# Splitting the four index scatters of a token tile around the softmax product on GpSimd

## Chip, cores and metric

One core of one Trainium2 chip. The metric is the device time of one execution of the whole kernel in microseconds (us). Three timed runs of the kernel before gave 1762.08, 1763.48 and 1767.51 us; the median is 1763.48 us.

## The reference

Two residual blocks follow each other on 16 x 1024 tokens of width 512.

```python
x = x + attention(layernorm(x), ctx)   # 8 heads of 64, 64 context rows a batch, softmax over the rows
x = x + ffn(layernorm(x))              # 32 experts, top 4 by sigmoid score + bias, capacity 512 each,
                                       # weights normalised over the 4, plus a shared gated ffn
```

The part that matters here: every token is filed under its four experts in a table of slots (32 experts x 512 places), from which the expert stage later gathers its rows. The softmax of a tile needs, for each of 8 heads, the exponentials of 64 scores divided by their sum.

## The kernel before, in words

The 16,384 tokens are 128 tiles of 128. The kernel has a token stage, which is a software pipeline of steps n = 0 to 136, and an expert stage behind it. In a step every engine runs a fixed list of pieces, each for another tile: a piece with the lag L works on tile n - L. Each engine takes its list in order, and semaphores order the engines against each other. No planner is involved; the order within a step is the order in which the step function of each engine is written.

The pieces of one step that matter, by engine (the lags are the constants at lines 59 to 61):

- TensorE (PE): the scores of tile n-8 into S_ps (L485), the mix of tile n-10 into O_ps from the transposed probabilities pt_h and pt_l (L500), the router logits of tile n-14 (L517); twice in a group of four tiles the upper half of the shared ffn (L527) and twice its lower half (L537), and parts of the folded weights (L583, L599).
- ScalarE (ACT): the high part xt_h of the turned input of tile n-7 (L758), the rows x and x_h of tile n-13 (L846, L858), the first guess of an inverse root (L862), the high part p_h of the probabilities of tile n-9 (L788), the exponentials prob of tile n-8 (L799).
- VectorE (DVE): in even steps the first piece of a root iteration (L1033, a tensor_scalar on four elements a lane) at the head of the step; the low parts x_l of tile n-13 (L1221) and p_l of tile n-9 (L1227), the row maxima (L1280), the difference from them (L1286), the sums of the exponentials (L1298) and their reciprocals rsum of tile n-8 (L1314), then pieces of the shared ffn (L1084, L1089, L1116) and of the routing.
- SyncE (SP): the DMA queue. In a step it turns x_h and x_l (L397), then p_h and p_l (L404).
- GpSimd (POOL): first the low part xt_l of tile n-7 (L932); in two of four steps the low part ht_l of the shared ffn's hidden rows (L940), which the lower half of that ffn on PE and VectorE's next copy stand beside; then four indirect DMAs (L923), one for each of the four expert slots of each token of tile n-20; then the product prob = prob x rsum of tile n-8 (L947).

The function `file(t, first, end)` issues the indirect DMAs of the slots first to end-1 of tile t. The first DMA of a group of four tiles waits until the slots of the group are there (`slots_ready`). The product waits for `rsum_done`.

In the text below, steps are told apart by n mod 4. The group pieces fall as follows: ht_l on GpSimd in steps with n mod 4 of 2 and 3; the slot list of the next group (L1199, L1206, L1211, L1212) on VectorE in mod 3 (L1199 at its head); the residuals of the shared ffn (L1116) at the end of mod 3 and mod 0; the root's first piece L1033 at the head of mod 0 and mod 2. In some steps with mod 3 PE also projects keys and values for a later pair of batches (L566, function `kv`); between step 23 and step 131 there are 28 steps with mod 3, 12 with that job and 16 without it. Those 16, with the mod 0 step behind each, are called free pairs below.

Of the kernel before, what the change touches and what calls it, by code (L numbers as in the profile page):

```python
# [36 lines left out]
E, TOP, CAP, I = 32, 4, 512, 256  # L37
# [23 lines left out]
ROUTE, MEMBERS, SLOTS_AT, WEIGHTS, OUT, W_STORE, TABLE = 17, 18, 19, 20, 20, 21, 20  # L61
# [9 lines left out]
def at(n, lag):  # L71

    t = n - lag
    return t if 0 <= t < TILES else None


def group_at(n, lag):

    g = (n - lag) // 4
    return g if (n - lag) % 4 == 0 and 0 <= g < GROUPS else None  # L80
# [42 lines left out]
def after(eng, sem, count):  # L123

    if count > 0:
        eng.wait_ge(sem, count)
# [8 lines left out]
def tokens_and_experts(nc, x, xT, ctxT, wqT, wk, wv, wo, bo, gateT, bias, w1, w3, w2, sw1T, sw3T, sw2T, out, x2aug, table):  # L135
    stack = ExitStack()
    with stack:
# [201 lines left out]
        with nc.Block() as block:  # L339
# [571 lines left out]
            def _(pool):  # L911
                def file(t, first, end):
                    if t is None:
                        return
                    g, i = t // 4, t % 4
                    if i == 0 and first == 0:
                        if g == 0:
                            pool.wait_ge(fill_stored, (2 * PAD // P + 1) * 16)
                            pool.wait_ge(const_set, 11)
                        pool.wait_ge(slots_ready, 2 * g + 2)  # L920
                        pool.sem_inc(passed, 1)
                    for q in range(first, end):
                        pool.indirect_dma_start(  # L923
                            table, bass.IndirectOffsetOnAxis(ap=slot[:, g % 2, i, q:q + 1], axis=0),
                            tok_line[:, g % 2, i, :], None, bounds_check=SLOTS - 1, oob_is_err=False).then_inc(scattered[g % 2], 16)

                def step(n):
                    t = at(n, XT_SPLIT)
                    if t is not None:
                        pool.wait_ge(xt_hi, t + 1)  # L930
                        after(pool, scores_done, t - 1)
                        pool.tensor_tensor(xt_l[:, t % 2, :, :], xt[:, t % 2, :, :], xt_h[:, t % 2, :, :].bitcast(F32),  # L932
                                           ALU.subtract).then_inc(xt_lo, 1)
                    for c in range(2):
                        g = group_at(n, FFN_UP + c + 1)
                        if g is not None:
                            pool.wait_ge(ht_hi, g * 2 + c + 1)
                            after(pool, g_done, g * 4)
                            after(pool, u_done, g * 4)
                            pool.tensor_tensor(ht_l[:, c, :], hid[:, :], ht_h[:, c, :].bitcast(F32),  # L940
                                               ALU.subtract).then_inc(ht_lo, 1)
                    if n != FINAL + SCORES:
                        file(at(n, TABLE), 0, TOP)
                    t = at(n, SCORES)
                    if t is not None:
                        pool.wait_ge(rsum_done, t + 1)
                        pool.tensor_tensor(prob[:, t % 2, :, :], prob[:, t % 2, :, :],  # L947
                                           rsum[:, :].unsqueeze(2).to_broadcast([P, H, SKV]), ALU.mult).then_inc(prob_done, 1)
                    if n == FINAL + SCORES:
                        file(at(n, TABLE), 0, TOP)  # L950

                pool.memset(zrow, 0.0).then_inc(zero_set, 1)
                pool.memset(kbd[:, :, :, :], 0.0).then_inc(zero_set, 1)
# [24 lines left out]
                for n in range(TAIL):  # L978
                    step(n)
# [819 lines left out]
```

## Time and profile before

| | us |
|---|---|
| median of the three timed runs | 1763.48 |
| span of the profiled execution, first to last instruction | 1810.0 |
| token stage with filing, about | 130 to 1250 |
| last tiles, change of stage, about | 1250 to 1370 |
| expert stage, about | 1370 to 1810 |

The profiled execution is the only one whose instructions are seen. For it no time is shown apart from the span; the span is 46.5 us, 2.6%, above the median of the timed runs. Rows of instructions read: start, duration, engine, line, operation, out<-in; in brackets the idle time of the engine before it and who ended it.

### The profile page before, as it was taken

How to read it: one execution, taken by the hardware profiler on the slowest of the kernel's cores; microseconds unless marked ns; L12 is line 12 of the kernel's file. 1: busy time of each engine (PE TensorE's matmuls, PEld its weight loads, DVE VectorE, ACT ScalarE, POOL GpSimd, SP SyncE). 2: the span in 40 equal slices, each digit the busy share in tenths (PEclk: the TensorE clock that was granted, in tenths of full speed). 3: DMA queues.
4: the chain of work that ended last, by engine and by line, in shares of the span. 5: the costliest groups of instructions: out<-in, count | busy, mean ns of one | idle time of the engine just before them, and what ended most of it. 6: DMA issues, size and time to landing. Idle time of an engine off the chain costs nothing.

```text
span 1810.0 us, 31933 instructions
## 1 busy us (share of the span) xinstructions
PE 1641.8 (91%) x9056; PEld 1023.7 (57%) x9056; DVE 1378.9 (76%) x3486; ACT 1066.3 (59%) x2368; POOL 1252.4 (69%) x1104
## 2 busy tenths in 40 slices
PE   6999999999999999999999999999447999999991
PEld 4565656666566665656666565655224555555550
DVE  4678988987898897889779789898425777777771
ACT  4777766776776676777767767765213444444440
POOL 2337777777777777777767677777475787777874
PEclk8999999999999999999999999999678999999996
DMA  7557876667776666677666577777249889988665
GB/s 247 144 135 166 193 163 151 174 155 154 181 183 152 162 168 155 174 167 178 164 149 170 152 182 171 161 191 170 61 142 264 139 172 166 208 190 167 103 85 79
DMA packets 474532, 293.75 MB, mean 162 GB/s; under 512 B 342643, under 2 KB 385397, under 8 KB 474356
## 3 DMA queue, kind: packets, MB, share of 16 engines
q1 hardware_dynamic: 429300, 239.03, 51.9%
q0 software_dynamic: 45056, 52.67, 18.5%
q8 instruction: 74, 1.21, 0.3%
q14 instruction: 102, 0.84, 0.2%
HBM read 135.06 MB, written 110.17 MB: 135 GB/s over the span
## 4 chain that ended last, share of the span: by engine, by line
PE 45%; issue 17%; DVE 16%; ACT 9%; another core or an unknown queue 4%; DMA 3%; POOL 2%; SPq 2%; DVEq 0%; ACTq 0%; POOLq 0%
PE O_ps L500 9%; PE S_ps L485 8%; PE GE_ps L1580 5%; PE UE_ps L1580 4%; PE G_ps L527 4%; PE YE_ps L1620 4%; PE U_ps L527 3%; PE PREP_ps L583 2%; POOL out L1557 2%; PE PREP_ps L566 2%; DVE top_s L1280 2%; DVE x_l L1221 1%; DMA pt_l<-p_l 1%; PE TE_ps L1606 1%
## 5 line engine op out<-in xcount | busy, mean ns | idle before, releaser
L923 POOL DMA_INDIRECT slot_table<-tok_line,slot x480 | 507.7, 1058 | 132.0 <-issue 128.1
L932 POOL TENSOR_TENSOR xt_l<-xt,xt_h 128x512 fp32r<-128x512 f32 x128 | 164.6, 1286 | 179.5 <-ACT xt_h L758 179.5
L799 ACT ACTIVATE prob<-S_ps,rs 128x512 f32<-128x512 f32 x128 | 88.0, 688 | 257.3 <-DVE S_ps L1286 166.5
L485 PE MATMUL S_ps<-a_h,xt_h 128*128 128x512 f32 x512 | 213.3, 417 | 2.4 <-DVE m_l L1259 2.4
L500 PE MATMUL O_ps<-m_h,pt_h 128*128 128x512 f16 x512 | 195.9, 383 | 20.0 <-DMA pt_l<-p_l 18.9
L485 PE MATMUL S_ps<-a_h,xt_l 128*128 128x512 f32 x512 | 202.1, 395 | 0.0
L485 PE MATMUL S_ps<-a_l,xt_h 128*128 128x512 f32 x512 | 202.0, 395 | 0.0
L500 PE MATMUL O_ps<-m_h,pt_l 128*128 128x512 f16 x512 | 194.7, 380 | 0.0
L500 PE MATMUL O_ps<-m_l,pt_h 128*128 128x512 f16 x512 | 194.6, 380 | 0.0
L947 POOL TENSOR_TENSOR prob<-prob,rsum 128x512 f32<-128x512 f32 x128 | 135.4, 1058 | 83.0 <-DVE rsum L1314 62.3
L1557 POOL DMA_INDIRECT out<-ye,idx_far x80 | 126.3, 1579 | 52.2 <-issue 27.7
L485 PEld LDWEIGHTS S_ps<-a_h,xt_h 128*128 128x128 f32 x512 | 98.1, 192 | 37.4 <-issue 16.1
L1672 ACT ACTIVATE xe_h<-TE_ps 128x512 f16<-128x512 f32 x128 | 75.8, 593 | 67.7 <-PE TE_ps L1606 51.6
L1654 ACT ACTIVATE the<-GE_ps 128x512 f32<-128x512 f32 x64 | 38.2, 597 | 126.7 <-PE GE_ps L1580 90.5
L1221 DVE TENSOR_TENSOR x_l<-x,x_h 128x512 f16<-128x512 f32 x126 | 86.4, 685 | 33.4 <-ACT x_h L858 26.7
L1620 PE MATMUL YE_ps<-down_w,he_h 128*128 128x512 f32 x256 | 110.8, 433 | 0.6 <-DVE he_l L1712 0.6
L485 PEld LDWEIGHTS S_ps<-a_h,xt_l 128*128 128x128 f32 x512 | 97.5, 190 | 21.9
L500 PEld LDWEIGHTS O_ps<-m_h,pt_h 128*128 128x128 f16 x512 | 49.9, 97 | 102.9 <-issue 29.5
L485 PEld LDWEIGHTS S_ps<-a_l,xt_h 128*128 128x128 f32 x512 | 98.0, 191 | 17.3
L1606 PE MATMUL TE_ps<-ident_r,rows 128*128 128x128 f32 x512 | 67.2, 256 | 43.9 <-DVE xe_l L1718 34.1
L846 ACT ACTIVATE x<-xr,nb,rs 128x512 f32<-128x512 f32 x128 | 102.8, 803 | 1.0 <-DVE nb L1045 1.0
L1700 DVE SCALAR_TENSOR_TENSOR gte<-the,GE_ps 128x512 f32<-128x512 f32 x64 | 44.0, 688 | 77.5 <-ACT the L1654 49.8
(245 smaller groups left out, 4848.8 us busy)
## 6 DMA issues: line engine op xcount, KB each, us to landing
xt<-in_xT SPq DMA_DIRECT2D x128, 256.0 KB
xr<-in_x SPq DMA_DIRECT2D x64, 512.0 KB, 3.8
x2aug<-x SPq DMA_DIRECT2D x128, 256.0 KB
out<-xr SPq DMA_DIRECT2D x64, 512.0 KB, 3.2
up_more<-in_w SPq DMA_DIRECT2D x36, 256.0 KB
slot_table<-tok_line,slot POOLq DMA_INDIRECT x512
up_w<-in_w SPq DMA_DIRECT2D x28, 256.0 KB
down_more<-in_w SPq DMA_DIRECT2D x18, 256.0 KB
```

The costliest lines, as they stand in the source:

```text
L485: last = pe.matmul(S_ps[t % 2][:, :], left[:, kc, :], right[:, b % 2, kc, :], start=(m == 0), stop=(m == 3 * KD - 1))
L500: last = pe.matmul(O_ps[:, :], left[:, t % 2, p, :], right[:, b % 2, p, :], start=(m == 0), stop=(m == 3 * PAIRS - 1))
L527: last = pe.matmul(bank[:, :], up_sb[:, kc, w0 + c * P:w0 + (c + 1) * P], part[:, g % 2, kc, :], start=(m == 0), stop=(m == 2 * KD - 1))
L799: act.activation(prob[:, t % 2, :, :], S_ps[t % 2][:, :].rearrange("p (h j) -> p h j", h=H), ACT.Exp, scale=rs[:, q % 2, 0, t % 2:t % 2 + ...
L846: act.activation(x2[:, t % 2, :], x_tile(t), ACT.Identity, bias=nb2[:, q % 2, t % 2:t % 2 + 1], scale=rs[:, (q + LATER) % 2, 1, t % 2:t % ...
L923: pool.indirect_dma_start(table, bass.IndirectOffsetOnAxis(ap=slot[:, g % 2, i, q:q + 1], axis=0), tok_line[:, g % 2, i, :], None, bounds_ ...
L932: pool.tensor_tensor(xt_l[:, t % 2, :, :], xt[:, t % 2, :, :], xt_h[:, t % 2, :, :].bitcast(F32), ALU.subtract).then_inc(xt_lo, 1)
L947: pool.tensor_tensor(prob[:, t % 2, :, :], prob[:, t % 2, :, :], rsum[:, :].unsqueeze(2).to_broadcast([P, H, SKV]), ALU.mult).then_inc(pro ...
L1221: dve.tensor_tensor(split_rows(t)[1][:, :], x2[:, t % 2, :], split_rows(t)[0][:, :], ALU.subtract).then_inc(x2_lo, 1)
L1557: pool.indirect_dma_start(out, bass.IndirectOffsetOnAxis(ap=index(e, c), axis=0), ye[:, e % 4, c, :], None, bounds_check=TOKENS + PAD - 1, ...
L1580: last = pe.matmul(bank[:, :], up_set(e)[:, kc, w0 + c * P:w0 + (c + 1) * P], part[:, e % TURNED, kc, :], start=(n == 0), stop=(n == 2 * K ...
L1620: last = pe.matmul(YE_ps[i % 2][:, :], part[:, e % 2, c, i * P:(i + 1) * P], down_w[:, e % 2, c, :], start=(n == 0), stop=(n == 2 * KI - 1))
```

## The change

GpSimd's list in a step is cut differently. Two of the four indirect DMAs of tile n-20 stay ahead of the product of tile n-8, the other two are issued behind it, and so stand ahead of the next step's xt_l. The one step in which all four stood behind the product (n = FINAL + SCORES = 135) stays as it is. Nothing is removed or added: the same instructions with the same operands and the same semaphores.

```diff
@@ -940,7 +940,7 @@
                             pool.tensor_tensor(ht_l[:, c, :], hid[:, :], ht_h[:, c, :].bitcast(F32),
                                                ALU.subtract).then_inc(ht_lo, 1)
                     if n != FINAL + SCORES:
-                        file(at(n, TABLE), 0, TOP)
+                        file(at(n, TABLE), 0, 2)
                     t = at(n, SCORES)
                     if t is not None:
                         pool.wait_ge(rsum_done, t + 1)
@@ -948,6 +948,8 @@
                                            rsum[:, :].unsqueeze(2).to_broadcast([P, H, SKV]), ALU.mult).then_inc(prob_done, 1)
                     if n == FINAL + SCORES:
                         file(at(n, TABLE), 0, TOP)
+                    else:
+                        file(at(n, TABLE), 2, TOP)
```

## Rows read from the trace of the kernel before

**Rows 1.** Windows, us 130 to 1250: PE, PEld, DVE, ACT, POOL, clock, DMA.

```profile
130.00:1250.00 1120.00, 1096.15 (x6232) 686.83 (x6231) 960.89 (x2701) 786.35 (x1845) 827.27 (x748) 1.00 0.70 168
```

**Rows 2.** Waits of PE in that window: us in total, times, longest.

```profile
PE O_ps L500 <- DMA pt_l<-p_l: 12.0, 14, 1.6
```

**Rows 3.** Groups by line: busy us, mean ns, idle before, releaser.

```profile
L788 ACT ACTIVATE p_h<-prob 128x512 f16<-128x512 f32 x128 | 78.5, 613 | 0.0
```

**Rows 4.** Timeline of GpSimd, end of step 70 and step 71.

```profile
628.83 0.97 POOL L923 DMA_INDIRECT slot_table<-tok_line,slot  x1 [0.30 <-issue]
629.80 1.08 POOL L947 TENSOR_TENSOR prob<-prob,rsum 128x512 f32<-128x512 f32 x1
631.67 1.28 POOL L932 TENSOR_TENSOR xt_l<-xt,xt_h 128x512 fp32r<-128x512 f32 x1 [0.79 <-ACT xt_h L758]
632.90 1.28 POOL L940 TENSOR_TENSOR ht_l<-hid,ht_h 128x512 fp32r<-128x512 f32 x1
```

**Rows 5.** Timeline of VectorE in the same stretch.

```profile
628.67 0.19 DVE L1314 RECIPROCAL rsum<-sums 128x8 f32<-128x8 f32 x1
...
633.37 0.86 DVE L1211 COPY tok_line<-tok 128x64 int32<-128x64 int32 x1
...
634.22 0.68 DVE L1221 TENSOR_TENSOR x_l<-x,x_h 128x512 f16<-128x512 f32 x1
```

**Rows 6.** Timeline of GpSimd, step 39.

```profile
318.63 1.28 POOL L932 TENSOR_TENSOR xt_l<-xt,xt_h 128x512 fp32r<-128x512 f32 x1 [1.89 <-ACT xt_h L758]
```

**Rows 7.** Timeline of GpSimd, end of step 71 and step 72.

```profile
639.61 1.08 POOL L947 TENSOR_TENSOR prob<-prob,rsum 128x512 f32<-128x512 f32 x1
640.61 1.30 POOL L932 TENSOR_TENSOR xt_l<-xt,xt_h 128x512 fp32r<-128x512 f32 x1
642.07 1.01 POOL L923 DMA_INDIRECT slot_table<-tok_line,slot  x1 [0.17 <-issue]
```

**Rows 8.** Timeline of VectorE in the same stretch.

```profile
638.26 0.20 DVE L1314 RECIPROCAL rsum<-sums 128x8 f32<-128x8 f32 x1
...
639.62 2.33 DVE L1033 TENSOR_SCALAR nt<-mv 128x4 f32<-128x4 f32 x1
...
642.52 0.67 DVE L1221 TENSOR_TENSOR x_l<-x,x_h 128x512 f16<-128x512 f32 x1
643.12 0.15 DVE L1036 TENSOR_TENSOR nt<-rs 128x4 f32<-128x4 f32 x1
```

**Rows 9.** Timeline of ScalarE in the same stretch.

```profile
641.26 0.63 ACT L858 ACTIVATE x_h<-x 128x512 f16<-128x512 f32 x1
```

**Rows 10.** Line L1033: ns shortest/median/longest, first and last start.

```profile
L1033 DVE TENSOR_SCALAR nt<-mv x67: 159/915/2346, 25.4 to 1289.9; 128x4 f32<-128x4 f32 x67
```

**Rows 11.** Timeline of VectorE and GpSimd, end of step 72.

```profile
647.35 0.19 DVE L1314 RECIPROCAL rsum<-sums 128x8 f32<-128x8 f32 x1
...
647.63 1.04 POOL L947 TENSOR_TENSOR prob<-prob,rsum 128x512 f32<-128x512 f32 x1 [0.73 <-issue]
```

**Rows 12.** Timeline of GpSimd and VectorE, step 131.

```profile
1214.43 1.27 POOL L940 TENSOR_TENSOR ht_l<-hid,ht_h 128x512 fp32r<-128x512 f32 x1
...
1214.45 1.29 DVE L1212 TENSOR_SCALAR slot<-slot_f 128x16 int32<-128x16 f32 x1
```

**Rows 13.** Timeline of GpSimd and VectorE, step 133.

```profile
1230.05 1.31 POOL L932 TENSOR_TENSOR xt_l<-xt,xt_h 128x512 fp32r<-128x512 f32 x1
...
1230.93 0.98 DVE L1221 TENSOR_TENSOR x_l<-x,x_h 128x512 f16<-128x512 f32 x1 [1.40 <-ACT x_h L858]
```

**Rows 14.** Timeline of VectorE and GpSimd, step 83.

```profile
746.89 0.29 DVE L1199 TENSOR_TENSOR over<-taken,member 128x128 f32<-128x128 f32 x1
...
746.96 1.38 POOL L932 TENSOR_TENSOR xt_l<-xt,xt_h 128x512 fp32r<-128x512 f32 x1 [0.72 <-ACT xt_h L758]
```

**Rows 15.** Timeline of PE: first product of the mix, steps 41 and 72.

```profile
335.83 0.39 PE L500 MATMUL O_ps<-m_h,pt_h 128*128 128x512 f16 x1 [0.77 <-DMA pt_l<-p_l]
...
641.37 0.39 PE L500 MATMUL O_ps<-m_h,pt_h 128*128 128x512 f16 x1 [0.92 <-DMA pt_l<-p_l]
```

## The prediction, on record before the change was run

> **What bounds the kernel now.** I read the windows first. In the token stage with filing PE is busy 1096 of 1120 us at the full clock [rows 1], so the stage runs at PE's pace, and any other engine matters only where it makes PE wait. The change lies wholly in this stage. Next the waits of PE in that window: the mix waits 14 times for the transposed low probabilities pt_l, 12.0 us in all [rows 2]. So the chain that can reach PE is VectorE's p_l, its transposition on SP, and the mix. Then the groups by line: ScalarE's p_h, the only reader of the product that the change moves, has no idle time ahead of it in 128 cases [rows 3]. The product is never awaited. Making it earlier is worth nothing by itself; what counts is what the move does to GpSimd's other pieces, and to VectorE, which the last reading, the timelines of the two engines side by side, shows to stop where GpSimd works.
>
> Three such stops are to be seen. The copy L1211 lasts 0.86 us and ends (634.23) with GpSimd's ht_l (634.18); x_l starts there, at 634.22 [rows 4, 5]. The root piece L1033 takes 0.16 us at its shortest [rows 10] but 2.33 us in step 72, where it starts with the product (639.61) and ends just behind the xt_l that follows (641.91) [rows 7, 8]; the 16 free pairs all show 2.31 to 2.35. And x_l, with two inputs in SBUF, takes 0.98 instead of 0.68 us where an xt_l is still running [rows 13, 5].
>
> **The change, step by step.** Nothing is removed or added; two of four indirect DMAs a step go behind the product. Each costs GpSimd 0.97 us and a gap of 0.30 [rows 4], the first behind a tensor operation 1.01 and a gap of 0.17 [rows 7].
>
> *The product.* In step 70 rsum ends at 628.86 and the last DMA starts at 628.83 [rows 4, 5]; the second ended two DMAs with gaps, about 1.6 us, before rsum. GpSimd will then stand at the wait for rsum, and the product starts as it does in step 72, where it already is so: 0.09 us behind rsum (647.54 to 647.63) [rows 11]. Behind the waiting product stand the other two DMAs and the next xt_l. Gain on the path: 0, since p_h doesn't wait [rows 3].
>
> *The DMAs behind it.* From rsum the next xt_l can start at 0.09 + 1.06 (product) + 0.17 + 1.01 + 0.30 + 0.97 = 3.60 us. Their landing in the table is awaited by nobody before the expert stage.
>
> *xt_l and ht_l of mod 3.* Now xt_l starts 631.67 - 628.86 = 2.81 us behind rsum [rows 4, 5], when ScalarE's xt_h is there. It will start at 3.60, so 0.79 later, and ht_l right behind it also. xt_l itself is for scores a whole step later and is covered by that step. ht_l isn't covered: VectorE's copy of the slot list will end with xt_l rather than with ht_l, but the next piece, L1212, then meets ht_l, as in step 131, where it took 1.29 us beside an ht_l of 1.27 [rows 12]. So x_l again starts where ht_l ends, 0.79 us later, and the maxima, p_l and pt_l behind it in VectorE's and SP's order. In mod 3 steps with the key job PE has so much to do ahead of the mix that I count nothing. In three of the 16 free ones xt_l already starts 3.9 to 4.1 behind rsum, as in step 39, where the idle time ahead of it is 1.89 and not 0.79 [rows 6, 4]: nothing there. 13 x 0.79 = 10.3 us, from 0 (all inside PE's slack) to 10.3.
>
> *L1033 at the head of mod 0.* It starts 639.62 - 638.46 = 1.16 us behind rsum [rows 8]; the product will run from 0.09 to 1.15 and be over. L1033 falls from 2.33 to 0.16: 2.17 us freed 16 times, 35 us of VectorE's time. But x_l behind it needs ScalarE's x_h, which ends 641.89, 3.43 us behind rsum [rows 8, 9]. x_l starts at 3.47 rather than 4.06. Of the 2.17 us 0.59 is left.
>
> *xt_l at the head of mod 0.* It starts 2.15 us behind rsum now (640.61) and will ask for its start at 3.60, in the midst of x_l (3.47 to 4.15). This collision is new. GpSimd does wait for VectorE: in step 83 xt_l beside L1199, two inputs in SBUF, took 1.38 instead of 1.28 [rows 14, 4]. VectorE's next piece, the small product L1036, comes at 4.07. In the nearest case, ht_l waiting behind the copy and L1212 next on VectorE, GpSimd went first [rows 12]. I take that: xt_l runs from about 4.05 to 5.33, and L1036 ends at about 5.35 instead of 4.81 (643.27) [rows 8]. The 0.59 gain turns into a loss of 0.54: 16 x 0.54 = 8.6 us. Lower end: VectorE runs through its queue, -0.59 x 16 = -9.4. Upper end: xt_l gets in before x_l, which then starts at 4.88 rather than 4.06: 0.82 x 16 = 13.1.
>
> The Trainium skill (SBUF — State Buffer, section Who interferes with whom) speaks against this change: a VectorE operation with two SBUF inputs and a GpSimd operation that reads SBUF exclude each other, and "Issue order, not op shape, decides who blocks". By that rule xt_l, issued before L1036, goes first and the sum is that of the forecast; without it the sum is that of the first rival. The row of step 83 agrees that GpSimd waits for such an operation.
>
> *mod 1 and mod 2.* xt_l in the step behind mod 0 is later too, but p_l there is not what PE waits for in most cases; nothing is counted.
>
> **The sum.** On the profiled execution 10.3 + 8.6 = 18.9 us. PE waits in only 14 mixes [rows 2], though two of those are in the places in question (0.92 us behind step 71 and 0.77 behind step 40, a mod 0 step) [rows 15]; the other places have some slack. I take off a quarter for it, a choice: 14 us. The profiled execution is 46.5 us longer than the median of the runs; I put the 14 us on the median: 1763.5 + 14 = 1777.5, 0.8% slower.
>
> **The rivals.**
>
> *VectorE isn't stopped by the moved xt_l.* Its small products L1036 and L1172 slip in between x_l and xt_l. Then p_l of mod 0 comes at +0.79 - 0.59 = +0.20, and PE loses between 10.3 - 9.4 = 1 us and what the mod 3 steps lose in themselves after slack, about 6. For it: L1036 is a row of 0.15 us. Against it: rows 12. About 1767, within 0.3% for the most part. Chance 0.14.
>
> *Everything is hidden.* The 0.79 us are within the slack of all mixes: 1763.5. Against it: the mix behind step 71 waits already [rows 15]. Chance 0.08.
>
> *Faster.* One mechanism: the freed L1033. If ht_l's lateness stays off the path and x_l gains its 0.59 us in mod 0, PE gets back its waits behind those steps. They are at most the 12.0 us of all waits; by PE's timeline 6 of the 14, 0.55 to 1.26 us each and 5.2 in sum, lie behind the mod 0 step of a free pair, the one in step 41 among them [rows 2, 15]: 1758. It decides as soon as xt_l of mod 0 begins behind L1036, and ht_l of mod 3 begins at most 0.2 us later than now. For it: 2.33 us is the largest single stop on VectorE [rows 8]. Against it: the 3.60 us are a plain sum of rows. Chance 0.12.
>
> **How the numbers follow.** The forecast has 0.66. About 0.3%, 5.3 us, is what a measurement of this kernel can tell from no change (the runs shown spread by that much). Slower: 0.66 and 0.03 of the first rival, 0.69. Same: 0.11 of the first rival and 0.08, 0.19. Faster: 0.12. The range goes from just below the fast rival, 1757, to the upper ends without slack, 10.3 + 13.1 = 23.4, so 1787; of the slow cases it is 1767 to 1787.
>
> **What will show it.** The product starts about 0.1 us behind rsum in every step, and the idle time ahead of it grows. xt_l of mod 3 starts 3.6 us behind rsum, and x_l where ht_l ends. No L1033 of 2.33 us is left in the free pairs; if there are any, the product is not over at 1.15. L1036 at the head of mod 0 is stretched to a microsecond or more; if it stays at 0.15, the first rival holds. PE's waits for pt_l rise from 12.0 by some 14 us; if they fall, the fast rival holds. The forecast is wrong if ht_l doesn't move, or moves and x_l doesn't follow, or PE has more slack than the quarter.

## The result, and the profile after

The changed kernel takes 1808.64 us in the median (1807.82 to 1811.03, 4 runs), the kernel before 1762.78 us (1761.09 to 1767.51, 4 runs) beside it. The ratio is 1.0249, with an interval of 1.0236 to 1.0262: slower by 2.5%, 46 us by the medians and 43.9 by the ratio. The forecast was 1777.5 us, 14 us slower; the direction was right, the size a third of what came, and the time lies above the range.

The profiled execution of the changed kernel has a span of 1806.0 us. The execution of before whose rows stand above (span 1810.0) was one long execution; a second profile of the unchanged kernel, run later beside the experiments, has a span of 1762.7 us, with the same three stops of VectorE in the same places. Totals of after are compared with that second profile, called the second before. VectorE's lines stand 2 higher in the changed kernel (rsum L1316, x_l L1223, the root piece L1035), GpSimd's as before. Mean granted clock is 1.00 between 130 and 1230 us in both, so the clock has no part in it.

First the windows, second before and after, the same 1100 us: PE, PEld, DVE, ACT, POOL, clock, DMA.

```profile
130.00:1230.00 1100.00, 1090.67 (x6221) 684.81 (x6220) 958.11 (x2690) 785.52 (x1842) 825.20 (x746) 1.00 0.73 171
```

```profile
130.00:1230.00 1100.00, 1060.82 (x6019) 662.03 (x6017) 973.53 (x2604) 756.53 (x1792) 802.12 (x719) 1.00 0.67 165
```

In the same time VectorE gets through 2604 instructions instead of 2690, 3.2% fewer, and yet is busy for longer; PE is idle 39 us instead of 9. The whole stage slows: from the first row maximum (L1280, now L1282) to the last it takes 1236.9 us instead of 1197.3, 39.6 of the 43.3 us between the two spans.

Next the waits of PE between 130 and 1250 us (us in total, times, longest), second before:

```profile
PE O_ps L500 <- DMA pt_l<-p_l: 10.7, 14, 2.0
```

After:

```profile
PE O_ps L500 <- DMA pt_l<-p_l: 23.8, 30, 2.5
PE G_ps L537 <- issue: 11.8, 12, 1.9
```

The mix waits for pt_l 23.8 us in 30 places, where it was 10.7 in 14 (12.0 in 14 in the long execution [rows 2]). The second line is new: the lower half of the shared ffn on PE is ready before GpSimd's ht_l is. The wait is put down to "issue", but all 12 of these start 0.10 us behind the end of an ht_l, as this one does, whose ht_l ends at 639.51 in the timeline of GpSimd below:

```profile
639.61 0.47 PE L537 MATMUL G_ps<-down_sb,ht_h 128*128 128x512 f32 x1 [0.59 <-issue]
```

Then the groups by line, second before: busy us, mean ns, idle before.

```profile
L1033 DVE TENSOR_SCALAR nt<-mv 128x4 f32<-128x4 f32 x67 | 69.2, 1033 | 22.0 <-ACT waste L742 12.7 <-issue 8.3 <-ACT waste L719 1.0
...
L1221 DVE TENSOR_TENSOR x_l<-x,x_h 128x512 f16<-128x512 f32 x126 | 87.5, 694 | 35.7 <-ACT x_h L858 35.7
...
L1211 DVE COPY tok_line<-tok 128x64 int32<-128x64 int32 x32 | 27.6, 861 | 1.1
```

The same after, with the product:

```profile
L947 POOL TENSOR_TENSOR prob<-prob,rsum 128x512 f32<-128x512 f32 x128 | 133.4, 1042 | 249.6 <-DVE rsum L1316 244.2
...
L1035 DVE TENSOR_SCALAR nt<-mv 128x4 f32<-128x4 f32 x67 | 36.5, 545 | 17.8 <-issue 16.1 <-ACT waste L719 1.0 <-ACT waste L742 0.6
...
L1223 DVE TENSOR_TENSOR x_l<-x,x_h 128x512 f16<-128x512 f32 x126 | 146.5, 1163 | 43.9 <-ACT x_h L858 43.9
...
L1213 DVE COPY tok_line<-tok 128x64 int32<-128x64 int32 x32 | 50.9, 1592 | 1.1
```

Here is the account. The root piece gives 69.2 - 36.5 = 32.7 us of VectorE back, as forecast. But x_l takes 146.5 - 87.5 = 59.0 us more, and the copy of the slot list 23.3. Three pieces that compute the same as before cost VectorE 49.6 us more in the run. And the product, now issued early in every step, only waits longer for rsum (249.6 us idle ahead of it), while its reader p_h still waits for nothing (0.0 ahead of L788, as in [rows 3]).

Where the 59 us lie is seen in the timelines. First GpSimd of after, from the end of step 70 to the head of step 73:

```profile
633.52 1.04 POOL L947 TENSOR_TENSOR prob<-prob,rsum 128x512 f32<-128x512 f32 x1 [1.72 <-DVE rsum L1316]
634.72 1.00 POOL L923 DMA_INDIRECT slot_table<-tok_line,slot  x1 [0.16 <-issue]
636.02 0.97 POOL L923 DMA_INDIRECT slot_table<-tok_line,slot  x1 [0.31 <-issue]
637.01 1.28 POOL L932 TENSOR_TENSOR xt_l<-xt,xt_h 128x512 fp32r<-128x512 f32 x1
638.24 1.27 POOL L940 TENSOR_TENSOR ht_l<-hid,ht_h 128x512 fp32r<-128x512 f32 x1
...
647.38 1.29 POOL L932 TENSOR_TENSOR xt_l<-xt,xt_h 128x512 fp32r<-128x512 f32 x1
...
653.66 1.04 POOL L947 TENSOR_TENSOR prob<-prob,rsum 128x512 f32<-128x512 f32 x1 [2.29 <-DVE rsum L1316]
...
657.14 1.29 POOL L932 TENSOR_TENSOR xt_l<-xt,xt_h 128x512 fp32r<-128x512 f32 x1
```

VectorE of after in the same stretch:

```profile
633.23 0.20 DVE L1316 RECIPROCAL rsum<-sums 128x8 f32<-128x8 f32 x1
...
637.86 1.71 DVE L1213 COPY tok_line<-tok 128x64 int32<-128x64 int32 x1
639.49 0.16 DVE L1214 TENSOR_SCALAR slot<-slot_f 128x16 int32<-128x16 f32 x1
639.57 0.68 DVE L1223 TENSOR_TENSOR x_l<-x,x_h 128x512 f16<-128x512 f32 x1
...
643.61 0.20 DVE L1316 RECIPROCAL rsum<-sums 128x8 f32<-128x8 f32 x1
...
644.96 0.17 DVE L1035 TENSOR_SCALAR nt<-mv 128x4 f32<-128x4 f32 x1
...
647.26 1.96 DVE L1223 TENSOR_TENSOR x_l<-x,x_h 128x512 f16<-128x512 f32 x1 [0.61 <-ACT x_h L858]
649.15 0.15 DVE L1038 TENSOR_TENSOR nt<-rs 128x4 f32<-128x4 f32 x1
...
653.38 0.19 DVE L1316 RECIPROCAL rsum<-sums 128x8 f32<-128x8 f32 x1
...
656.76 2.23 DVE L1223 TENSOR_TENSOR x_l<-x,x_h 128x512 f16<-128x512 f32 x1 [0.61 <-ACT x_h L858]
...
660.23 0.68 DVE L1229 SCALAR_TENSOR_TENSOR p_l<-prob,p_h 128x512 f16<-128x512 f32 x1
```

And of the second before, the last step of that stretch (rows of both engines in order of time; the same step, 14.6 us earlier in the run):

```profile
638.73 0.19 DVE L1314 RECIPROCAL rsum<-sums 128x8 f32<-128x8 f32 x1
...
640.22 1.27 POOL L932 TENSOR_TENSOR xt_l<-xt,xt_h 128x512 fp32r<-128x512 f32 x1 [0.17 <-ACT xt_h L758]
...
642.11 0.69 DVE L1221 TENSOR_TENSOR x_l<-x,x_h 128x512 f16<-128x512 f32 x1 [0.61 <-ACT x_h L858]
...
644.05 0.68 DVE L1227 SCALAR_TENSOR_TENSOR p_l<-prob,p_h 128x512 f16<-128x512 f32 x1
```

The reader is to see three steps, each counted from the end of its rsum. In step 71 (mod 3) xt_l starts 3.58 behind rsum (637.01 - 633.43), ht_l ends at 6.08, and copy and x_l follow it: as forecast. In step 72 (mod 0) xt_l starts at 3.57 and meets x_l, which takes 1.96 us instead of 0.68. In step 73 (mod 1) the move does the same again: xt_l went from 1.30 behind rsum, where it was over before x_l was due, to 3.57, and x_l, ready at 3.19, takes 2.23 us instead of 0.69. p_l comes 6.66 behind rsum instead of 5.13. In the whole run x_l took over 1.9 us in no step of the second before and in 37 of after, 22 of them over 2.1; in all 37 it ends 0.56 us behind the GpSimd piece that held it.

The mean time of a step, from one row maximum to the next, over steps 22 to 130, by n mod 4, worked out from the starts in each trace, shows what it comes to:

| kernel | mod 0 | mod 1 | mod 2 | mod 3 | sum |
|---|---|---|---|---|---|
| second before | 7.90 | 11.05 | 9.99 | 9.32 | 38.26 |
| after | 9.12 | 10.80 | 10.52 | 9.25 | 39.70 |

The mod 0 step, which ends behind that x_l of step 73, grew by 1.22 us. No other step grew as much. The 1.22 is a mean of two kinds: of the 27 mod 0 steps from 24 to 128, the 21 whose x_l was held grew by 1.53 to 1.65 us, the other six not at all (there x_l starts 2.24 or 2.25 behind rsum and is over before xt_l). The row maximum follows x_l without a pause in all of them, before and after, so the step grows by the whole of the stop.

### The profile page after: what moved, and what is told of

The parts are those of the page before. It is cut to its first block and busy times, and to the rows that moved or that the text cites. A ratio compares the mean times of both kernels' runs of the same rounds, so it can differ in the third digit from the quotient of the medians.

```text
span 1806.0 us, 31933 instructions
## 1 busy us (share of the span) xinstructions
PE 1643.4 (91%) x9056; PEld 1021.8 (57%) x9056; DVE 1430.4 (79%) x3486; ACT 1060.7 (59%) x2368; POOL 1259.5 (70%) x1104
## 5 line engine op out<-in xcount | busy, mean ns | idle before, releaser
L923 POOL DMA_INDIRECT slot_table<-tok_line,slot x480 | 515.6, 1074 | 117.2 <-issue 116.2
L947 POOL TENSOR_TENSOR prob<-prob,rsum 128x512 f32<-128x512 f32 x128 | 133.4, 1042 | 249.6 <-DVE rsum L1316 244.2
L1223 DVE TENSOR_TENSOR x_l<-x,x_h 128x512 f16<-128x512 f32 x126 | 146.5, 1163 | 43.9 <-ACT x_h L858 43.9
L1720 DVE TENSOR_TENSOR xe_l<-TE_ps,xe_h 128x512 f16<-128x512 f32 x128 | 87.7, 688 | 30.6 <-ACT xe_h L1674 28.9
L1731 DVE TENSOR_SCALAR ye<-YE_ps,rows 128x512 f32<-128x512 f32 x128 | 95.4, 746 | 11.9 <-PE YE_ps L1622 10.6
```

The lines of the kernel that those rows point to most:

```text
L923: pool.indirect_dma_start(table, bass.IndirectOffsetOnAxis(ap=slot[:, g % 2, i, q:q + 1], axis=0), tok_line[:, g % 2, i, :], None, bounds_ ...
L1223: dve.tensor_tensor(split_rows(t)[1][:, :], x2[:, t % 2, :], split_rows(t)[0][:, :], ALU.subtract).then_inc(x2_lo, 1)
L1731: dve.tensor_scalar(ye[:, e % 4, i, :], YE_ps[i % 2][:, :], w, None, ALU.mult).then_inc(y_read, 1)
```

## The experiments

Each kernel's time is told as its ratio to the kernel before, run on the same chip (medians 1763.65 to 1764.48 us there), with the interval; us are the ratio less 1, times 1763. Edits of the first kind below change only how many of the four DMAs stand ahead of the product, by n mod 4, in the two calls of `file`:

```python
file(at(n, TABLE), 0, (a, b, c, d)[n % 4])      # ahead of the product
...
file(at(n, TABLE), (a, b, c, d)[n % 4], TOP)    # behind it
```

(4, 4, 4, 4) is the kernel before, (2, 2, 2, 2) the change. The DMAs behind the product of a mod 0 step delay the xt_l at the head of the mod 1 step, and so on. Two causes were set against each other: that VectorE's pieces are held by the moved xt_l, and that the lateness of GpSimd's own pieces, ht_l and xt_l, costs by itself.

**The kernel before once more.** No edit.

> The kernel before, unchanged, for a second profile of it. The first profiled execution had a span of 1810.0 us although the timed runs give 1762.8. If that execution was merely a long one, the new span lies about 1761, the token stage (first to last row maximum on VectorE, 1213 us in the first profile) is shorter by up to 23 us and the rest, from the last p_h to the end, by 26 us. If the profile itself makes this kernel longer, the span is again about 1810 while the time beside it is 1763.

Measured: 0.9996 (0.9981 to 1.0012). It gives the second before.

**The change without mod 0**, (4, 2, 2, 2), **and mod 0 alone**, (2, 4, 4, 4).

> The changed kernel, but in steps with n mod 4 = 0 all four index DMAs stay ahead of the product. Theory A: the loss is x_l of the mod 1 steps, held by the moved xt_l (2.23 instead of 0.69 us, 1.53 us in each of 28 groups); the ring of four VectorE steps falls from 39.78 to 38.25 us, below PE's pace, so nearly all of the 46 us comes back: 1763 to 1772. Theory B (the prediction: the later ht_l and the held x_l of mod 0 carry the loss, mod 1 nothing): nothing comes back, 1803 to 1809. If the three losses simply add: 1809 less some 43, but no lower than before.

> The kernel before with the split in steps with n mod 4 = 0 alone. Theory A (mod 1's x_l is the loss by itself): 1.53 us x 28 = 43 us of VectorE's time, of which PE's slack takes some: 1785 to 1806. Theory B: within 5 us of before, 1758 to 1768. If VectorE only paces the stage when all losses together push its ring of four steps over PE's 38.9 us: ring 38.3, so 1763 to 1772.

Measured: 1.0090 (1.0055 to 1.0125) without it, 1.0111 (1.0076 to 1.0145) with it alone. So the split of the mod 0 step, for which the prediction counted nothing, costs 19.6 us by itself, and 28.0 (43.9 - 15.9) where the others are split too: the largest part either way. Without it the mod 0 step is back at 7.93 us, with it alone it takes 9.14. Between the change and the kernel without mod 0 only this step is longer in the change, 9.12 against 7.93; the other three are shorter by 0.02 to 0.14, and the xt_l of mod 2 starts 3.61 behind rsum in the median of both. So what the mod 0 split adds to the others lies in the one step with the held x_l. With mod 0 alone a second thing comes in: six DMAs stand between the products of steps 72 and 73, the product of mod 1 starts 1.16 behind rsum in the median instead of 0.50, and xt_l and the ht_l behind it in mod 2 start later as well, xt_l at 4.24 instead of 3.75, when ScalarE's xt_h is there. How much of the 19.6 us that makes up no run shows. GpSimd and VectorE of the kernel with mod 0 alone, head of step 73:

```profile
649.13 1.30 POOL L932 TENSOR_TENSOR xt_l<-xt,xt_h 128x512 fp32r<-128x512 f32 x1
...
648.73 2.25 DVE L1223 TENSOR_TENSOR x_l<-x,x_h 128x512 f16<-128x512 f32 x1 [0.61 <-ACT x_h L858]
```

The same stop, alone, with the other steps as before; x_l sums to 120.6 us there, 33.1 over the second before.

**The change without mod 2**, (2, 2, 4, 2).

> The changed kernel, but in steps with n mod 4 = 2 all four index DMAs stay ahead of the product, so that ht_l of the mod 3 steps comes no later than before. Theory A: ht_l's part is 0.78 us of a ring of 39.78, 28 times, 22 us at most: 1787 to 1800. Theory B: ht_l is the larger of the two terms, more than half comes back: 1763 to 1785.

Measured: 1.0136 (1.0108 to 1.0165), 24.0 us over before. The mod 2 step falls from 10.52 to 9.79 us (ht_l is no longer late there), the mod 0 step stays at 9.14. x_l still takes 144.0 us in all.

**The two late DMAs of mod 0 put behind the next xt_l.** The same split and the same product as in the change, but xt_l of mod 1 no longer stands behind the DMAs.

```python
# in step(n), behind xt_l and ht_l
if n % 4 == 1:
    file(at(n - 1, TABLE), 2, TOP)
...
# behind the product, in place of the else
elif n % 4 or n == TAIL - 1:
    file(at(n, TABLE), 2, TOP)
```

> The changed kernel, with one order turned round: the two index DMAs that a mod 0 step puts behind its product are issued behind the next step's xt_l instead of ahead of it. The number of DMAs behind the product stays. Theory X (x_l is held by xt_l, which these two DMAs push into it): xt_l of mod 1 starts 1.3 us behind rsum again, x_l there takes 0.69 us instead of 1.9 to 2.2, and about as much comes back as with mod 0 whole, 26 us of 46: 1778 to 1787. Theory D (the DMAs themselves hold x_l): x_l stays at 1.5 us or more, the time at 1803 to 1810.

Measured: 1.0217 (1.0200 to 1.0234), 38.3 us. By the time alone the theory of the held x_l fails; the trace says otherwise. GpSimd, steps 73 and 74 (the product is L949, VectorE's lines 4 higher than before):

```profile
656.36 1.27 POOL L932 TENSOR_TENSOR xt_l<-xt,xt_h 128x512 fp32r<-128x512 f32 x1 [0.17 <-ACT xt_h L758]
...
663.01 1.07 POOL L949 TENSOR_TENSOR prob<-prob,rsum 128x512 f32<-128x512 f32 x1
...
666.55 1.30 POOL L932 TENSOR_TENSOR xt_l<-xt,xt_h 128x512 fp32r<-128x512 f32 x1
667.77 1.29 POOL L940 TENSOR_TENSOR ht_l<-hid,ht_h 128x512 fp32r<-128x512 f32 x1
```

VectorE in the same stretch:

```profile
658.26 0.69 DVE L1225 TENSOR_TENSOR x_l<-x,x_h 128x512 f16<-128x512 f32 x1 [0.61 <-ACT x_h L858]
...
666.49 2.61 DVE L1037 TENSOR_SCALAR nt<-mv 128x4 f32<-128x4 f32 x1
```

x_l of mod 1 is back at 0.69 us, and the mod 0 step at 7.90. But with four DMAs ahead of it in step 73 the product is 0.50 late, and the xt_l behind it starts within 0.06 us of the root piece, which is held through xt_l and ht_l, 2.61 us; 26 root pieces take over 2 us in this kernel, against 1 in the change. The mod 1 step goes from 10.80 to 11.81, which takes nearly all of it back. What this kernel shows is both: freeing x_l frees the step, and at this other place the two DMAs bring xt_l onto another of VectorE's pieces (the xt_l of mod 2 starts 4.03 behind rsum in the median, 3.61 in the change).

**Mod 3 alone**, (4, 4, 4, 2), **and mod 2 alone**, (4, 4, 2, 4): the two terms that the prediction did count, the x_l at the head of mod 0 and ht_l of mod 3.

> The kernel before with the split in steps with n mod 4 = 3 alone. VectorE's L1033 of mod 0 falls from 2.33 to 0.16 us, and x_l there is held by xt_l until 4.87 us behind rsum. Prediction's step (a net loss of 0.54 us in each of 16 free pairs): p_l of mod 0 0.7 us later, 1768 to 1776. If the steps of the free pairs are VectorE's and the loss is 0.7 us a pair: 11 us, 1771 to 1777. If the freed L1033 wins: 1755 to 1760.

> The kernel before with the split in steps with n mod 4 = 2 alone, that is ht_l of mod 3 later by 0.79 us and nothing else. If it costs by itself as in the prediction (13 to 28 times 0.79 us less slack): 1772 to 1784. If it counts only when the ring of four steps is already over PE's pace: 1761 to 1769. The step with mod 2 should take about 0.75 us longer in the free groups in either case.

Measured: mod 3 alone 1.0071 (1.0046 to 1.0096), 12.5 us; mod 2 alone 1.0042 (1.0026 to 1.0057), 7.4 us. GpSimd and VectorE with mod 3 alone, head of step 72:

```profile
636.03 1.28 POOL L932 TENSOR_TENSOR xt_l<-xt,xt_h 128x512 fp32r<-128x512 f32 x1
...
633.60 0.17 DVE L1035 TENSOR_SCALAR nt<-mv 128x4 f32<-128x4 f32 x1
...
635.91 1.96 DVE L1223 TENSOR_TENSOR x_l<-x,x_h 128x512 f16<-128x512 f32 x1 [0.62 <-ACT x_h L858]
```

The freed root piece and the held x_l stand in one step. Summed over the run the root pieces are 34.3 us shorter than in the second before and x_l only 23.1 longer, and yet the kernel is slower: VectorE spends most of the freed time waiting for ScalarE. In the median the x_l of mod 0 starts 3.47 instead of 4.08 behind rsum, but ends at 5.43 instead of 4.76. With mod 2 alone ht_l ends 6.2 us behind rsum, x_l follows at once, and the mod 2 step takes 10.54 us instead of 9.99.

**Mod 1 alone**, (4, 2, 4, 4).

> The kernel before with the split in steps with n mod 4 = 1 alone. There xt_l of mod 2 starts 3.6 us behind rsum already, as the sum of rows gives for the split, so nothing moves: 1760 to 1768. If the four single splits add up to the whole (20 + 8 + mod 3 + mod 1 = 46 us) and mod 3 gives 11, this one has 7: 1768 to 1773.

Measured: 1.0005 (0.9993 to 1.0017): nothing. There ScalarE's xt_h is late anyway (it ends 3.53 us behind rsum, as in the kernel before), so the DMAs delay nothing.

**One DMA behind the product in mod 3 only**, (4, 4, 4, 3), and the same with ht_l issued ahead of xt_l. One DMA is enough to take the product off the root piece and too short to bring xt_l onto x_l.

> The kernel before with one index DMA, not two, behind the product, in steps with n mod 4 = 3 alone. The product starts 0.09 us behind rsum, L1033 at the head of mod 0 falls from 2.33 to 0.16 us, and xt_l runs from 2.33 to 3.6 us behind rsum, ahead of x_l (3.45). If VectorE's gain of some 0.6 us in 16 free pairs reaches PE: 1755 to 1761. If x_l is again caught by xt_l (held to 3.6 and 0.55 more): 0.4 us gained at most, 1758 to 1766. If it is all hidden: as before, within 5 us.

> As the kernel with one DMA behind the product in mod 3, and ht_l ahead of xt_l on GpSimd in the steps with mod 2 and 3. ht_l's input is there before xt_l's, so the pair of them starts some 0.5 us earlier and x_l, L1212 and PE's lower half follow earlier. If the steps with mod 2 and 3 pace the stage together with PE: 5 to 12 us faster than before, 1752 to 1758. If PE's pace is the floor: within 5 us of before. If ScalarE's ht_h comes late, xt_l waits behind it and nothing is gained or some us are lost.

Measured: 0.9989 (0.9976 to 1.0001), and with ht_l first 0.9985 (0.9975 to 0.9996), 2.6 us faster than before: the best version found, at 0.15% (0.04 to 0.25). VectorE and GpSimd of the first, head of step 72:

```profile
629.81 0.17 DVE L1035 TENSOR_SCALAR nt<-mv 128x4 f32<-128x4 f32 x1
...
632.12 0.70 DVE L1223 TENSOR_TENSOR x_l<-x,x_h 128x512 f16<-128x512 f32 x1 [0.62 <-ACT x_h L858]
...
630.97 1.28 POOL L932 TENSOR_TENSOR xt_l<-xt,xt_h 128x512 fp32r<-128x512 f32 x1
```

Both stops are gone from this step, yet the run gains hardly more than can be told apart.

**One DMA moved along in every step**: in mod 1 and mod 3 the last DMA goes behind the product, in mod 0 behind the next xt_l.

```python
if n % 4 == 1:
    file(at(n - 1, TABLE), 3, TOP)
...
file(at(n, TABLE), 0, (3, 3, 4, 3)[n % 4])
...
elif n % 4 or n == TAIL - 1:
    file(at(n, TABLE), (3, 3, 4, 3)[n % 4], TOP)
```

> The kernel before with single DMAs moved so that no tensor operation of GpSimd meets x_l: in mod 3 the fourth DMA goes behind the product, in mod 0 the fourth goes behind the next step's xt_l, in mod 1 the fourth goes behind the product. L1033 of mod 0 takes 0.16 us, x_l 0.7 in mod 0 and 0.69 in mod 1, the product starts at most 0.5 us behind rsum. If VectorE paces the free pairs: 0.55 us less in each of 16, 9 us: 1752 to 1758. If PE's pace is the floor there: 1759 to 1765.

Measured: 1.0003 (0.9992 to 1.0015). The windows show why (the same 1100 us as above):

```profile
130.00:1230.00 1100.00, 1093.66 (x6240) 687.07 (x6239) 932.81 (x2704) 788.53 (x1849) 835.52 (x749) 1.00 0.72 171
```

No root piece takes over 2 us and no x_l over 1.9, VectorE is busy 25 us less than in the second before, and the time is the same: PE is busy 1093.7 of 1100 us. Stops taken from VectorE buy nothing here, since PE sets the pace; that stops added to it are paid is what the kernels above show.

## Why the prediction was right in direction and wrong in size

*Right.* The product starts 0.08 to 0.09 us behind rsum in every step (653.57 to 653.66 in step 72), and being earlier is worth nothing. xt_l starts 3.57 to 3.59 behind rsum at the heads of mod 3 and mod 0; 3.60 was summed from rows. ht_l of step 71 is 0.77 later than in [rows 4], 0.79 forecast, and x_l follows it. One detail is other: it is the copy that is held to the end of ht_l (1.71 us), not L1212 behind it. The root piece falls from 2.33 to 0.17. xt_l at the head of mod 0 meets x_l, and the small product behind it (L1036, now L1038) ends 5.49 us behind rsum, 5.35 forecast.

*Right in size, another way.* The forecast let x_l run and L1036 wait for xt_l. In fact x_l itself is held (1.96 us) and the small product takes its 0.15; that its end came within 0.14 us of the forecast is luck. By the prediction's own sign, L1036 at 0.15, the first rival would hold; it doesn't, because the stop lies one piece earlier. Of the rule of the Trainium skill (SBUF — State Buffer, section Who interferes with whom) the trace agrees that the two exclude each other. That issue order decides it does not show: by the profile x_l started at 647.26, before xt_l at 647.38, and was held all the same. No run here tells whether the profile's start is the issue that the page means.

*The two counted terms.* 10.3 us for ht_l of mod 3 measured 7.4 with that split alone, 8.6 for the head of mod 0 measured 12.5; together 19.9 against 18.9, with intervals of 4.6 to 10.0 and 8.1 to 16.9. The quarter that was taken off for PE's slack was, by these measurements, not there to take: 14 of 19.9. PE's waits for pt_l rose by 13.1 us, close to the 14 of the prediction's own sign, but PE was idle 29.9 us more in the 1100 us of the windows, 11.8 of it at L537, which the sum had no term for. A smaller slip of the working had no effect: the landing of the DMAs is awaited before the expert stage, by VectorE's slot list (L1211) two groups later, but the idle time ahead of that is 1.1 us in both.

*The step that failed* is "mod 1 and mod 2. xt_l in the step behind mod 0 is later too, but p_l there is not what PE waits for in most cases; nothing is counted." It moved by as much as at the head of mod 0, from 1.30 to 3.57 behind rsum, onto an x_l that is ready at 3.19. That costs 1.54 us at a time; the split that brings it costs 19.6 us when done alone and 28.0 in the change. Without it the change costs 15.9 us, where the forecast, which had left it out, said 14. The plain sum 0.09 + 1.06 + 0.17 + 1.01 + 0.30 + 0.97 = 3.60 holds for every step, and the working used it only at two of four heads. The reason given was true and doesn't carry: only 2 of the 14 waits of [rows 2] lie behind a p_l of mod 1. But that PE seldom waits for it says that it comes in time by some margin, not that the margin is 1.5 us; and VectorE, which takes its list in order, is then late for what follows, too. Told by the step of the p_l that was awaited, from each trace, PE's waits for pt_l between 130 and 1250 us were

| kernel | mod 0 | mod 1 | mod 2 | mod 3 |
|---|---|---|---|---|
| second before | 9, 5.3 us | 1, 2.0 us | none | 4, 3.4 us |
| mod 0 alone | 9, 5.2 us | 4, 3.7 us | 9, 4.6 us | 8, 5.1 us |

With mod 0 alone 13 of the 16 new waits lie one or two steps behind the one with the held x_l; PE waits another 3.8 us at L537. Some of this can come from GpSimd's own later pieces there instead of from VectorE.

*What the terms don't add up to.* The four splits alone cost 19.6, 0.9, 7.4 and 12.5, together 40.4 us; the change costs 43.9 by its ratio. Parts of it don't add either: mod 0, 1 and 3 cost 24.0 together, not 33.0; mod 1, 2 and 3 cost 15.9, not 20.8. With the intervals of all their terms, 8 to 9 us to either side, none of these three differences stands clear of the noise. One does: taking the mod 2 split out of the change gives back 19.9 us (43.9 - 24.0), though alone it costs 7.4. Late steps make each other dearer there. It fits that a step between two late ones can catch up, and that with all of them late none can: with mod 0 alone the mod 3 step takes 8.76 us against 9.32 in the second before, in the change 9.25. PE's wait at L537 grows in the same way, 11.8 us in the change, but 3.8 with mod 0 alone, 0.4 with mod 2 alone, 0.7 without mod 0 and 3.5 without mod 2. That this is the cause of the larger sum no run tested by itself; it stays open.

*The rivals.* "Everything is hidden" and "faster" fell with the first collision. The mechanism of the fast rival is real, though: with one DMA in place of two the root piece is freed and xt_l stays clear of x_l, and that was worth 1.9 to 2.6 us, not 5.2, because PE was busy 1090.7 of 1100 us to begin with.

## What to carry to other kernels

When a piece that shares a resource is shifted by a fixed amount, lay the shift over every step of the period, and ask at each what now runs beside it; a stop removed at one head (2.33 to 0.17 us) came back as a larger sum on the next piece there and at another head. That the bounding engine seldom waits for a chain gives no leave to count nothing for it: compare the new stop with the pause that the held engine has ahead of its next piece (here none), and follow its lateness into the steps behind. And where the bounding engine is busy 99%, stops taken off another engine can be worth almost nothing (25 us of VectorE's time for no gain) while stops added to it are paid in good part (33.1 us on x_l for 19.6 us with mod 0 alone).

## What the runs showed of the hardware

A VectorE piece with two inputs in SBUF that started ahead of a GpSimd piece, by the profile, was still held to that piece's end. x_l of step 73 starts at 656.76 and xt_l at 657.14, when more than half of x_l's usual 0.69 us was over; x_l ends at 658.99, 0.56 behind xt_l, and xt_l keeps its 1.29. In 36 of the 37 such cases of the change x_l starts 0.10 to 0.49 us ahead of xt_l, and it ends 0.56 behind the GpSimd piece every time: the head start, however long, shortens nothing. A tensor_scalar on four elements a lane was held through two GpSimd pieces in a row, 2.61 us for 0.17. By rows of GpSimd and of VectorE in the kernel with one DMA moved along, an indirect DMA beside x_l does not do this:

```profile
631.38 1.29 POOL L932 TENSOR_TENSOR xt_l<-xt,xt_h 128x512 fp32r<-128x512 f32 x1
632.84 1.26 POOL L923 DMA_INDIRECT slot_table<-tok_line,slot  x1 [0.17 <-issue]
...
632.53 0.69 DVE L1225 TENSOR_TENSOR x_l<-x,x_h 128x512 f16<-128x512 f32 x1 [0.62 <-ACT x_h L858]
```

There x_l, begun 0.14 us before xt_l ended, keeps its 0.69 and again ends 0.55 behind xt_l. The DMA's issue takes 1.26 there instead of 1.00, but a DMA later in the same run takes 1.33 with no x_l beside it, so that what stretches it is not shown. That the head start shortens nothing fits if a start in the profile is only the moment from which a VectorE piece asks to read, but no run here tests that.
